# Expert layer of a two-block transformer kernel: tokens packed by expert without padding, and the weight copies split between ScalarE and VectorE

## The reference, cut to what matters

```python
logits = xf @ gate_w + gate_b
one_hot = one_hot(argmax(logits, axis=-1), E)          # E = 8, one expert for each token
h = gelu(einsum('td,edh->teh', xf, w1), approximate=True)   # up product, HID = 512
y = einsum('teh,ehd->ted', h, w2)                           # down product
out = einsum('te,ted->td', one_hot, y)
```

## Time and profile before

| | |
|---|---|
| median of 3 runs | 903.89 us (903.69 to 904.23) |
| the profiled execution | 904.78 us |
| its span in the trace | 902.4 us |
| TensorE / VectorE / ScalarE / GpSimd busy, whole span | 802.4 / 751.3 / 636.4 / 242.4 us |
| first gather issued | 820.63 us |
| last result of the loop | 870.47 us |
| last scatter issued, landed | 880.66 us, 882.90 us |
| TensorE's granted clock, mean of the span | 0.948 |

### The profile page before, as it was taken

One profiled execution on the slowest core, in us unless ns is written; L12 is line 12 of the kernel. 1 busy time (PEld: TensorE's weight loads), 2 busy tenths in 40 slices (PEclk: granted clock), 3 DMA queues, 4 the chain that ended last, 5 costly groups with the idle time before them and its releaser, 6 DMA issues.

```text
span 902.4 us, 24156 instructions
## 1 busy us (share of the span) xinstructions
PE 802.4 (89%) x9661; PEld 308.1 (34%) x9661; DVE 751.3 (83%) x1195; ACT 636.4 (71%) x1267; POOL 242.4 (27%) x548
## 2 busy tenths in 40 slices
PE   5279999999999999999999999999999999955950
PEld 3013334333333333343333223322332322344950
DVE  4489988999999998889999998899999999236634
ACT  5037777777776777777778989999989999921311
POOL 3110413200000415232300543332011401004773
PEclk9559999999999999999999999999999999976985
DMA  3665444555555455346313333332321221101313
GB/s 88 185 194 176 144 138 161 170 177 172 171 176 175 137 165 171 117 158 202 108 50 110 107 112 101 102 92 76 93 66 55 61 81 53 31 16 50 51 53 99
DMA packets 69476, 104.78 MB, mean 116 GB/s; under 512 B 15845, under 2 KB 45861, under 8 KB 69365
## 3 DMA queue, kind: packets, MB, share of 16 engines
q1 hardware_dynamic: 62773, 68.30, 26.5%
q10 hardware_dynamic: 5120, 31.94, 9.9%
q0 software_dynamic: 1472, 3.02, 1.6%
HBM read 84.19 MB, written 18.87 MB: 114 GB/s over the span
## 4 chain that ended last, share of the span: by engine, by line
PE 69%; DVE 9%; POOL 6%; issue 4%; DMA 4%; ACT 4%; SPq 3%; POOLq 0%; DVEq 0%
PE bank L1304 23%; PE bank L1323 21%; PE bank L1330 12%; PE bank L1284 7%; DVE unit_max L1013 4%; ACT prob_mem L907 4%; POOL prob_mem L797 3%; POOL moe_out L803 2%; PE bank L1249 1%; DVE stats L956 1%; PE bank L1371 1%; DMA maxima_rows<-max_rows 1%; PE bank L1257 1%; DMA k_parts<-prob_mem 1%; DMA bias_parts<-prob_mem 1%
## 5 line engine op out<-in xcount | busy, mean ns | idle before, releaser
L907 ACT ACTIVATE prob_mem<-bank 128x512 f32<-128x512 f32 x1024 | 556.6, 597 | 137.8 <-PE bank L1330 115.1
L1284 PE MATMUL bank<-k_rows,q_rows 56*128 56x512 bf16 x1024 | 328.2, 392 | 22.2 <-DMA k_rows<-k_parts 12.7
L1323 PE MATMUL bank<-q_rows,k_rows 59*128 59x512 bf16 x1024 | 334.4, 385 | 5.4 <-DMA q_rows<-maxima_rows 1.9
L1009 DVE CUSTOM_DVE_ANT_1 no_use<-bank,w_moe 128x1024 bf16<-128x1024 f32 x256 | 305.6, 1219 | 30.8 <-PE bank L1284 27.7
L1304 PE MATMUL bank<-prob_mem,v_ring 128*32 128x256 f32 x4096 | 320.4, 386 | 7.8 <-issue 6.7
L1013 DVE TENSOR_REDUCE unit_max<-bank 128x1 f32<-128x1024 f32 x256 | 297.4, 1217 | 15.0 <-PE bank L1284 13.4
L1323 PEld LDWEIGHTS bank<-q_rows,k_rows 59*128 59x128 bf16 x1024 | 81.1, 93 | 243.2 <-ACT prob_mem L907 117.9
L708 POOL CAST max_parts<-unit_max 128x8 bf16<-128x8 f32 x64 | 12.1, 189 | 553.3 <-DVE unit_max L1009 312.8
L1304 PEld LDWEIGHTS bank<-prob_mem,v_ring 128*32 128x32 f32 x4096 | 102.6, 109 | 153.6 <-ACT prob_mem L907 60.5
L1330 PE MATMUL bank<-skew_mem,pick 96*32 96x512 bf16 x1664 | 138.3, 390 | 0.0
L1284 PEld LDWEIGHTS bank<-k_rows,q_rows 56*128 56x128 bf16 x1024 | 77.1, 93 | 32.7 <-DVE unit_max L1009 14.7
(11 more groups left out here) (181 smaller groups left out, 532.2 us busy)
## 6 DMA issues: line engine op xcount, KB each, us to landing
w_moe<-bias_rows ACTq DMA_DIRECT2D x31, 960.0 KB, 5.8
q_rows<-q_parts SPq DMA_DIRECT2D x252, 48.0 KB
k_rows<-k_parts SPq DMA_DIRECT2D x126, 96.0 KB
skew_mem<-bias_parts SPq DMA_DIRECT2D x32, 378.0 KB, 4.1
unit_sums<-o_ring SPq DMA_DIRECT2D x63, 128.0 KB, 2.3
w_moe<-in_L_ffn_w_dram SPq DMA_DIRECT2D x16, 256.0 KB, 3.0
q_parts<-prob_mem SPq DMA_DIRECT2D x8, 384.0 KB, 3.1
k_parts<-prob_mem SPq DMA_DIRECT2D x24, 128.0 KB, 2.7
```

The lines of the kernel that those rows point to most:

```text
L907: nc.scalar.activation(prob[:, kb, half * N:(half + 1) * N], b_bank(("exp", exp_no(n, kb, half))), ACT.Exp).then_inc(exp_done, 1)
L1009: nc.vector.tensor_tensor_reduce(out=no_use[:, qb % 2, :].rearrange("p (k c) -> p k c", k=QB), in0=scores.rearrange("p (k c) -> p k c", k= ...
L1284: return nc.tensor.matmul(sa_slot(QB * m + qb)[:, f, :], q_rows[rows, m % SLOTS, qb * P:(qb + 1) * P], k_rows[rows, m % SLOTS, f * N:(f + ...
L1323: return nc.tensor.matmul(b_bank(("exp", exp_no(n, kb, f))), k_rows[rows, n % SLOTS, kb * P:(kb + 1) * P], q_rows[rows, n % SLOTS, f * N:( ...
```

## The change

The tokens are put one behind another, ordered by expert, with no padding: 16 tiles are gathered and scattered instead of 23. A tile may then hold tokens of several experts. The loop runs over 23 pairs ("segments") of one tile and one expert. A segment computes the whole tile with its expert's weights, and its result is multiplied by a mask (`in_pair`, 1 for the rows of that expert) and added into `slot_y` of the tile. For this:

- The list of places is made from `first_slot`, the start of each expert in tokens. The tile counts are made later, and give `expert_u` and `tile_u` of each segment.
- ScalarE applies scale and shift once for each tile (`tile_features`, into `tile_feat`) and copies the up product's weights, 512 elements (`up_weights`).
- VectorE copies the down product's weights, 512 elements, and for each segment copies the tile's features into `slot_feat`.
- `slot_y` is set to zero by GpSimd before the gathers; scatter j waits for result `min(j + 8, 23)`.

The core of the diff:

```diff
-                nc.vector.tensor_copy(w_ring[:, j % 4, :], w_moe[:, bass.ds(e, 1), :].rearrange("p o w -> p (o w)")).then_inc(w_ready, 1)
+                nc.vector.tensor_copy(w_ring[:, j % 4, HID:WE], w_moe[:, bass.ds(e, 1), HID:WE].rearrange("p o w -> p (o w)")).then_inc(w_ready, 1)

             def result(j):
+                tile = dve.value_load(tile_u[0:1, j:j + 1], min_val=0, max_val=TT - 1)
                 dve.wait_ge(down_mm, j + 1)
-                nc.vector.tensor_copy(slot_y[:, j, :], bank[:, 4 + j % 2, 0:D]).then_inc(y_ready, 1)
+                if j:
+                    dve.wait_ge(y_ready, j)
+                rows = slot_y[:, bass.ds(tile, 1), :].rearrange("p o d -> p (o d)")
+                nc.vector.scalar_tensor_tensor(rows, bank[:, 4 + j % 2, 0:D], in_pair[:, j:j + 1], rows, ALU.mult,
+                                               ALU.add).then_inc(y_ready, 1)

             def features(j):
-                dve.wait_ge(slot_t_mm, j + 1)
+                tile = dve.value_load(tile_u[0:1, j:j + 1], min_val=0, max_val=TT - 1)
+                dve.wait_ge(feat_ready, min(j, TT - 1) + 1)
                 if j >= 4:
                     dve.wait_ge(up_mm, j - 3)
-                nc.vector.tensor_scalar(slot_feat[:, j % 4, :], bank[:, j % 2, 0:P], ln_par[:, 2:3], ln_par[:, 3:4],
-                                        ALU.mult, ALU.add).then_inc(slot_t_ready, 1)
+                nc.vector.tensor_copy(slot_feat[:, j % 4, :], tile_feat[:, bass.ds(tile, 1), :].rearrange("p o n -> p (o n)")
+                                      ).then_inc(slot_t_ready, 1)
...
             features(0)
+            chain(nc.vector.tensor_tensor(ended[:], ended[:], spread_ap(first_slot[:, :, :], [0, NS], [1, E]), ALU.mult))
+            chain(nc.vector.tensor_reduce(pair_start[:, 0:NS], ended[:], AX.X, ALU.max))
+            chain(nc.vector.scalar_tensor_tensor(pair_start[:, 0:NS], tile_f[:], float(P), pair_start[:, 0:NS], ALU.mult, ALU.max))
+            chain(nc.vector.tensor_scalar(pair_slot[:], tile_f[:], float(P), row_no[:, 0:1], ALU.mult, ALU.add))
+            chain(nc.vector.tensor_tensor(from_next[:], pair_slot[:], pair_start[:, 1:NS + 1], ALU.is_ge))
+            chain(nc.vector.tensor_tensor(in_pair[:], pair_slot[:], pair_start[:, 0:NS], ALU.is_ge))
+            chain(nc.vector.tensor_tensor(in_pair[:], in_pair[:], from_next[:], ALU.subtract))
+            dve.wait_ge(y_zeroed, 1)
...
+            def tile_features(t):
+                act.wait_ge(slot_t_mm, t + 1)
+                nc.scalar.activation(tile_feat[:, t, :], bank[:, t % 2, 0:P], ACT.Identity, scale=ln_par[:, 2:3],
+                                     bias=ln_par[:, 3:4]).then_inc(feat_ready, 1)
+
+            def up_weights(j):
+                e = act.value_load(expert_u[0:1, j:j + 1], min_val=0, max_val=E - 1)
+                if j >= 4:
+                    act.wait_ge(up_mm, j - 3)
+                nc.scalar.copy(w_ring[:, j % 4, 0:HID], w_moe[:, bass.ds(e, 1), 0:HID].rearrange("p o w -> p (o w)")).then_inc(w_up_ready, 1)
+
+            up_weights(0)
+            tile_features(0)
+            up_weights(1)
             for j in range(NS):
+                if j + 1 < TT:
+                    tile_features(j + 1)
+                if j + 2 < NS:
+                    up_weights(j + 2)
                 act.wait_ge(up_mm, j + 1)
...
-            for j in range(NS):
-                pool.wait_ge(y_ready, j + 1)
+            for j in range(TT):
+                pool.wait_ge(y_ready, min(j + E, NS))
```

More of the change, by code:

```diff
@@ L183, in sandwich_kernel @@
         place_in_tile = sb("place_in_tile", [P, TT])
[L184 to L188, removed]
+        numbers = sb("numbers", [P, TT, 2, TT + 1], bf16)
+        slot_sum = sb("slot_sum", [P, TT + 1])
+        slot_token = sb("slot_token", [P, TT])
+        token_u = sb("token_u", [P, TT], mybir.dt.uint32)
         ended = sb("ended", [P, NS, E])
@@ L292, in sandwich_kernel @@
         expert_known = sem("expert_known")
-        slots_loaded = [sem(f"slots_loaded{n}") for n in range(SINGLY + (NS - SINGLY + 1) // 2)]
+        slots_loaded = [sem(f"slots_loaded{n}") for n in range(SINGLY + (TT - SINGLY + 1) // 2)]
         slot_t_mm = sem("slot_t_mm")
         slot_t_ready = sem("slot_t_ready")
+        feat_ready = sem("feat_ready")
+        y_zeroed = sem("y_zeroed")
         tokens_known = sem("tokens_known")
         w_ready = sem("w_ready")
+        w_up_ready = sem("w_up_ready")
         up_mm = sem("up_mm")
@@ L752, in _ @@
                                           pattern=[[1, E], [-1, E]], channel_multiplier=0))
-            for dst, pattern, base, per_row in ((tile_start, [[P, NS + 1]], 0, 0), (tile_no, [[1, NS]], 0, 0),
+            for dst, pattern, base, per_row in ((tile_start, [[P, TT + 1]], 0, 0), (pair_no, [[1, NS]], 1, 0),
                                                 (next_tile_no, [[1, TT]], 1, 0), (row_no, [[0, 1]], 0, 1),
-                                                (col_no, [[1, P]], 0, 0), (spare_no, [[P, NS]], P + T, 1)):
+                                                (col_no, [[1, P]], 0, 0), (turn_no, [[1, NS], [-1, E]], 1, 0)):
                 chain(nc.gpsimd.iota(dst[:], pattern, base=base, channel_multiplier=per_row,
                                      allow_small_or_imprecise_dtypes=True))
+            chain(nc.gpsimd.memset(pair_start[:, NS:NS + 1], float(T)))
             pool.sem_inc(moe_consts_ready, 1)
@@ L793, in _ @@
             pool.wait_ge(tokens_stored, 16 * B)
-            pool.wait_ge(gather_known, 1)
-            for j in range(NS):
+            nc.gpsimd.memset(slot_y[:], 0.0).then_inc(y_zeroed, 1)
+            pool.wait_ge(tokens_known, 1)
+            for j in range(TT):
                 nc.gpsimd.indirect_dma_start(out=slot_rows[:, j, :], out_offset=None, in_=tokens_dram,
-                                             in_offset=bass.IndirectOffsetOnAxis(ap=gather_u[:, j:j + 1], axis=0)
+                                             in_offset=bass.IndirectOffsetOnAxis(ap=token_u[:, j:j + 1], axis=0)
                                              ).then_inc(slots_loaded[arrival(j)[0]], 16)
-            pool.wait_ge(tokens_known, 1)
-            for j in range(NS):
-                pool.wait_ge(y_ready, j + 1)
+            for j in range(TT):
+                pool.wait_ge(y_ready, min(j + E, NS))
                 nc.gpsimd.indirect_dma_start(out=moe_dram, out_offset=bass.IndirectOffsetOnAxis(ap=token_u[:, j:j + 1], axis=0),
@@ L1157, in _ @@
                                     spread_ap(place_in_tile[:, :], [1, TT], [0, P]), ALU.is_equal).then_inc(numbers_ready, 1)
-            nc.vector.tensor_tensor(numbers[:, :, 1, :], at_least[:], spread_ap(next_tile_no[:, :], [1, TT], [0, NS + 1]),
+            nc.vector.tensor_tensor(numbers[:, :, 1, :], at_least[:], spread_ap(next_tile_no[:, :], [1, TT], [0, TT + 1]),
                                     ALU.mult).then_inc(numbers_ready, 1)
+            chain(nc.vector.tensor_tensor(counts[:], spread_ap(first_slot[:, :, :], [1, E], [0, TT]),
+                                          spread_ap(tile_start[:, :], [0, E], [1, TT]), ALU.is_ge))
@@ L1162, in _ @@
+            chain(nc.vector.tensor_reduce(tiles_of[:], counts[:], AX.X, ALU.add))
             dve.wait_ge(numbers_mm, 1)
[L1163 to L1172, removed]
+            chain(nc.vector.tensor_copy(slot_sum[:], bank[:, 7, 0:TT + 1]))
@@ L1498, in down @@
             def down(j):
+                pe.wait_ge(w_ready, j + 1)
                 pe.wait_ge(gelu_done, j + 1)
```

71 lines of the change are left out of this document (40 added, 31 removed).

## The result

The changed kernel takes 906.68 us (median of 12 runs) against 903.84 us for the kernel before, measured beside it: 1.0036 times, 95% interval 1.0026 to 1.0046, so 2.3 to 4.2 us slower. The forecast was 904.9 from 903.89, a ratio of 1.001, with 902.6 to 906.1 as the range of its own case and 901.5 to 909.5 as the whole range. The measured time lies in the second and above the first.

What follows compares the result with a forecast made beforehand. GpSimd's gathers and scatters bound the kernel before; VectorE's register loads would bind after: nineteen turns of 2.42 us put the last result at 880.85, the last landing at 883.9, +1.0, so 904.9 us; range 901.5 to 909.5.

Steps and rivals of the forecast that it cites:

- its own case: In VectorE's loop, the register loads bind with turns of 2.30 to 2.48 us; 902.6 to 906.1 us, chance 0.48.
- What bounded the kernel before: GpSimd's 23 gathers and 23 scatters, 46 turns of 1.31 making 60 us; last scatter starts 9.9 us after the last result.
- The turn: VectorE's loop: three register loads of 0.75 us in sequence plus waits, 2.42 us, 0.5 longer than before.
- the open small terms: VectorE's turn: second waits free or 0.06 us each, result's address perhaps computed twice for 0.06 to 0.1; turn 2.27 to 2.55.
- rival of a longer turn: VectorE's loop: address computed twice and second waits in full, turn 2.55, 2.5 us more, 907.4 us; chance 0.26.
- The stalls of the sequencer: VectorE's loop: one stall like the one at 844.32, 0.62 where 0.25 is usual, adding 0.4 us.
- The start: Before the loop: token list and first up product 1.0 us earlier, with 0.5 of it left at the second up product.
- a clock that rises a step later: Loop start: TensorE's gap at 826 may delay its full clock a step; half of 1.0 us, 0.5, was added.
- The tail: After features(22): up product 1.05, Gelu 0.65, down product 1.05, result 0.35, with hand-overs 3.45 us to the last result.
- TensorE as the bound: Loop: loads overlap, turns under 2.27 us, last scatter lands at 872.5; 10.4 us less, 893.5 us; chance 0.13.
- The clock didn't fall: Rival in the loop: gaps drop TensorE's clock, five or six turns of 3.6 us add 7, 912 us; chance 0.10.
- The ring on ScalarE: Loop: ScalarE's load and copy bring the next Gelu 2.65 us after its predecessor's up product, covered since needed a turn later.

## Why the prediction was right, and where its sizes were off

**What bounded the kernel before** was right: with the loads added to its loop the last result moves by 4.5 us and the time by 0.15%; with 16 tiles moved the last scatter comes earlier by the 9.3 us of GpSimd's tail. (One sum in it is loose: 23 and 23 instructions have 45 steps from start to start, of 1.33 us, and not 46 of 1.31.)

**The turn** was the deciding term, and the mechanism held: three loads, one after another in VectorE's sequencer, 2.42 forecast and 2.46 measured. Of the open small terms, a second wait cost 0.07, above the 0.03 to 0.05 of the forecast and its upper 0.06 (0.84 with two waits for 0.77 to 0.78 with one), and the second address nothing (one step of 69 ns for both). So half of the rival of a longer turn came true and half did not. Over the 19 turns the difference makes 0.7 us. The floor of about 600 ns that the Trainium skill ("DMA: Bandwidth & Descriptors", "Latency and other measured facts") gives for a `tensor_load` is not the price here: a load was 303 ns, and one more of them with its arithmetic and check cost 0.61 a turn, in the fourth-load run.

**The stalls of the sequencer** were mis-sized. I put one of 0.4 us into the sum, from the one at 844.32. There are three: results stand 2.8 to 2.9 apart there in place of 2.45. That makes 1.3 us, 0.9 more than the forecast had. The line after one of them, and what the DMA queues carried from 857 to 858:

```profile
857.44 0.35 DVE L1217 SCALAR_TENSOR_TENSOR prob_mem<-bank,in_pair,prob_mem 128x128 f32 x1 [0.87 <-issue]
```

```profile
q14 instruction: 1, 0.01, 3.0%
```

The trace shows where they fall. Count all of VectorE's instructions in the trace, those of its sequencer too, from the first step of the places. The stalls come at number 107, 235 and 363, 128 apart, in the changed kernel and in the one with a fourth load; with two loads more in the kernel before at 107 and 235, and in the kernel before at 107. There number 235 lies behind the loop, at 892 us, so only one is seen. That is every seven or eight turns in the changed kernel and every six or seven with a fourth load. 0.7 to 1.0 us after each of the changed kernel's three, queue 14, of the kind "instruction", moves 8192 bytes; it has other transfers in between. That may point to the loading of instructions, but no run tests it. So the number of stalls could have been counted ahead: it grows with the instructions that the change adds to VectorE.

**The start** was 0.8 better than forecast, 1.8 us for the first up product in place of 1.0: GpSimd started its first gather 0.3 after the token list and not about 0.85, and the list was out another 0.2 sooner. The loop didn't keep it, since VectorE's masks and loads set the second segment. features(3) came 19.0 after the start of the places, where the forecast had it.

**The sum by the anchors.** The forecast's 880.85 for the last result is 69.3 after the start of the places (811.53); measured 70.7. The turns make 0.7 more and the stalls 0.9. The 0.5 for a clock that rises a step later was not needed: it came to full at 17.6, for 17.3 before. The tail, from features(22) to the end of the last result, took 3.8 for the forecast's 3.45. The sum has only a Gelu of 0.65 between the last up and the last down product; in the trace the down product of the segment before stands there, and the two run as one group:

```profile
882.09 2.03 PE L1545 MATMUL bank<-prob_mem 128*128 128x128 f32 x16
```

That these last two errors, 0.5 and 0.4, cancel is luck. The last scatter began 0.6 after the last result (0.8 forecast), so the load back is 2.2 later than before where 1.0 was forecast. The ratio gives 2.3 to 4.2, and the middle of it, 3.3, is not explained in full: the stretch behind the load is 0.4 longer in this profile (19.8 for 19.5), but the profile is of the slowest run, and in the experiments that stretch is 19.4 to 19.6.

**The range.** The measured 906.68 is 0.6 above the 902.6 to 906.1 that the forecast gave its own case, though its turn of 2.46 lies within 2.30 to 2.48. The sum was too low by 1.8 us, and it is the wider range, made for the longer turn and for more stalls, that holds the result. The single most likely answer by the prediction's chances, slower by more than 0.2% (0.43), is what came; the central number alone said "same".

**The ledger of the change**, in the profiles: 9.3 us saved by moving 16 tiles, 11.5 us lost on the last result, 2.2 left. Of the 11.5 the third load is 10.5 or more, since the kernel without it had the later clock; with it gone the last result is 1.0 later than before.

**The rivals.** TensorE as the bound was the outcome only with a load taken away. The clock didn't fall: 1.00 in both windows from 840 to 880, through 16 turns with a gap of 0.3 to 0.4 in each. The Trainium skill ("TensorE: Matmul & The Clock Gate", "A second HAM failure mode: psum-queue depth-cycling") tells of a kernel in which short idle times between groups made it go up and down; with these gaps it didn't here, nor with a fourth load, where TensorE was busy for 13.60 of 20 us at 1.00. The prediction's sentence that it rose only after a stretch without gaps doesn't hold: in the changed kernel TensorE was busy for 2.77 of the 3.40 us ahead of the rise (window above). Tables were loaded once in the loop, so Copy and Identity beside Gelu cost none. The ring on ScalarE, which I had called covered, was.

## What to carry to other kernels

Count the sequencer's work of an engine as a resource of its own: an instruction whose address comes from a register that was just loaded costs 0.75 to 0.85 us from start to start in these kernels, however short it is; the weight copy of 0.69 us hid most of that. Load an index once and keep the register for all its users: with the load done earlier, a register address cost no idle time. Count an engine's instructions as well, its sequencer's too: every 128 of them brought VectorE a stall of about 0.4 us here. When a queue elsewhere is the bound, first ask how much slack the next limit has: here 9.9 us, and 0.6 us in each of 20 turns spent more than that.

## What was not expected of the hardware

A small instruction whose address has just been loaded holds up the engine by more than its own length, yet the sequencer's parts are very constant (load 298 to 311 ns in `features`, arithmetic 190, check 23). Against that, the stalls of about 0.4 us are as regular, one in 128 instructions, and show as idle time "for issue" or as a wait for another engine that had long been done. And 20.00 of 20.00 us busy on TensorE was reached again with VectorE busy for 9.66 of them: busy shares alone would have ranked the changed kernel's VectorE as the freest engine after GpSimd.
